# Edge sort of a four-layer graph network: chunks of seven written-out steps in place of a ring of eight looped steps

## The reference, cut to what matters

```python
src, dst, attr, kind      # 412500 edges: source, destination (sorted), 16 attributes, one of 8 types
# layer 0: msg = emb[kind] @ x[src];            m = segment_sum(msg, dst); GRU cell
# layer 1: msg = x[src] @ (attr @ We + be);     segment_sum(msg, dst) + x + bias
# layer 2: two relational convolutions, each edge weighted by 1 / count(dst, kind)
# layer 3: a sheaf layer, sums by destination and by source
```

## Time and profile before

| | us |
|---|---|
| median of 3 runs | 16641.76 (16610.89 to 16656.3) |
| span of the profiled execution | 16996.1 |
| the sort in it, GpSimd's first scatter to its last | 310 to 6837, 6527 in all |
| layers behind it | about 10159 |
| GpSimd busy, the whole span | 5158.9 (30%) |
| VectorE busy, the whole span | 10824.2 (64%) |
| TensorE busy, the whole span | 11995.3 (71%) |

### The profile page before, as it was taken

How to read it: one execution, slowest core, us unless ns; L and a number is a source line. 1 busy time by engine, 2 the same in 40 slices (tenths; PEclk the granted TensorE clock), 3 DMA queues, 4 the chain that set the end, 5 groups by cost and what they waited for, 6 DMA issues and landing times. The chain is left out here.

```text
span 16996.1 us, 429738 instructions
## 1 busy us (share of the span) xinstructions
PE 11995.3 (71%) x146289; PEld 8312.1 (49%) x146290; DVE 10824.2 (64%) x19718; ACT 8088.7 (48%) x16130; POOL 5158.9 (30%) x4771
## 2 busy tenths in 40 slices
PE   1343443434434344799799998997996999999998
PEld 0111111111111111466688886665664888888887
DVE  3233333333333333688788887887886899999998
ACT  1232433433424234566466664665664555555554
POOL 1656666565664656000111111000000111111111
PEclk8555555555555555899899998999998999999999
DMA  7122222222222222688222222887885222333322
GB/s 208 48 72 59 81 67 66 81 59 71 74 58 79 58 72 82 184 229 229 89 106 106 106 106 95 234 235 198 235 235 126 80 83 83 85 85 84 84 84 71
DMA packets 1721891, 1905.31 MB, mean 112 GB/s; under 512 B 981549, under 2 KB 1429103, under 8 KB 1696207
## 3 DMA queue, kind: packets, MB, share of 16 engines
q1 hardware_dynamic: 1602775, 1863.79, 37.0%
q0 software_dynamic: 116864, 39.75, 1.5%
q10 hardware_dynamic: 2078, 0.15, 0.0%
HBM read 1449.57 MB, written 453.42 MB: 112 GB/s over the span
## 5 line engine op out<-in xcount | busy, mean ns | idle before, releaser
L688 POOL DMA_INDIRECT rec<-sort_ring,sort_idx x3520 | 4042.6, 1148 | 2791.9 <-issue 1469.7
L1381 DVE TENSOR_TENSOR e_full<-e_feats,e_masks 128x3840 bf16<-128x3840 bf16 x1179 | 2523.7, 2154 | 350.5 <-ACT e_feats L1339 302.0
L1294 PE MATMUL e_acc<-e_full,e_sel 128*128 128x384 bf16 (+1 forms) x11760 | 2120.9, 327 | 270.4 <-DVE e_full L1381 270.2
L778 PE MATMUL sort_ps_count<-sort_hot,upper_b 128*128 x400 | 231.6, 579 | 2689.9 <-DVE sort_hot L903 2144.6
L1530 PE MATMUL e_acc<-e_outer,e_sel 128*128 128x272 f32 x7840 | 1896.8, 397 | 3.9 <-DVE e_outer L1625 3.9
L1337 ACT CAST e_masks<-e_kind 128x1280 bf16<-128x1280 fp8e4 x1179 | 1482.6, 1258 | 629.5 <-DVE e_full L1381 575.0
L731 ACT CAST sort_cols_t<-sort_ps_late 120x256 f16<-120x256 f32 x98 | 39.5, 403 | 3439.8 <-remote 2373.0
L1530 PEld LDWEIGHTS e_acc<-e_outer,e_sel 128*128 128x128 f32 x7840 | 1459.2, 190 | 281.2 <-issue 4.1
L953 DVE TENSOR_TENSOR sort_over<-sort_ps_late,sort_late_base 128x20 f32<-128x20 f32 x175 | 30.7, 176 | 2428.1 <-remote 2208.7
L1294 PEld LDWEIGHTS e_acc<-e_full,e_sel 128*128 128x128 fp8e4 x11760 | 1061.0, 97 | 933.2 <-issue 298.1
L751 ACT ACTIVATE sort_made<-sort_ps_count,sort_window_bias 128x1024 fp8e4<-128x1024 f32 (+1 forms) x1274 | 1378.7, 1156 | 71.9 <-remote 26.7
(11 more groups left out here) (463 smaller groups left out, 22855.8 us busy)
## 6 DMA issues: line engine op xcount, KB each, us to landing
e_hot<-stream SPq DMA_DIRECT2D x888, 480.0 KB, 3.8
stream<-sort_made SPq DMA_DIRECT2D x98, 2568.0 KB
e_sel<-stream SPq DMA_DIRECT2D x1176, 160.0 KB, 2.7
e_st<-stream SPq DMA_DIRECT2D x99, 1888.0 KB, 7.3
sheaf_gather<-stream SPq DMA_DIRECT2D x393, 384.0 KB, 3.1
e_hot<-stream SPq DMA_DIRECT2D x294, 448.0 KB, 3.5
tail<-sort_made SPq DMA_DIRECT2D x98, 660.0 KB
sheaf_by_dst<-tail SPq DMA_DIRECT2D x491, 128.0 KB, 3.0
```

What stands on the lines that cost most here:

```text
L688: nc.gpsimd.indirect_dma_start(out=rec[q], out_offset=bass.IndirectOffsetOnAxis(ap=idx[:, s, q, c:c + 1], axis=0), in_=ring[:, s, q, c, :] ...
L1294: last = mm(acc[h][:, 0:cols_all], now[:, n * P:(n + 1) * P], full[q & 1][:, n, :], start=j == 0, stop=j == NT - 1)
L1381: v.tensor_tensor(full[q & 1][:, :, 0:cols].rearrange("p j (t k f) -> p j t k f", t=TYPES, k=3), feats[q & 1][:, :, :, :].unsqueeze(2).to_ ...
```

## The change

A quad's steps are done in chunks of `STEPS = 7`. The loop over steps becomes a loop over chunks, and in VectorE's, TensorE's and GpSimd's programs the seven steps of a chunk are written out. `ring`, `idx` and `keys` have two sides, each of 35 tiles for each of the four blocks, and GpSimd's loop takes two chunks in a round. The attributes lie in memory as the kernel's partitions take them, already 21 words wide, so that one DMA a block and chunk loads them (four a chunk); ScalarE writes the keys of the whole chunk with four instructions, and the one and the four fields with five. The pads go. `scattered` counts chunks. The last `find` of a quad, whose result nobody used, goes too. The rows of the odd blocks and their windows move to partitions 32 to 34 (`rows_all`, `windows`). Cut to its core:

```diff
-RING = 8
+STEPS = 7
+CT = STEPS * C
-        ring = sb("ring", [P, RING, Q, C, RW])
-        idx = sb("idx", [P, RING, Q, C], I32)
-        keys = sb("keys", [P, RING, Q, C])
+        ring = sb("ring", [P, 2, Q, CT, RW])
+        idx = sb("idx", [P, 2, STEPS, Q, C], I32)
+        keys = sb("keys", [P, 2, Q, CT])
-        rows = [sb(f"rows{h}", [3, NT, 2, P], F16) for h in range(2)]
+        rows_all = sb("rows", [SECOND + 3, NT, 2, P], F16)
+        rows = [rows_all[at:at + 3, :, :, :] for at in (0, SECOND)]
-        def place_of(i):
-            return bass.ds(i & (RING - 1), 1)
+        def side_of(i):
+            return bass.ds(i & 1, 1)
...
                         for q in range(Q):
-                            sp.dma_start(ring[:, place_of(i), q, :, 0:D].squeeze(1),
-                                         edges[:, tiles(t0[q] + local(i, i0) * C, C), :]).then_inc(attr_in, 16)
+                            sp.dma_start(ring[:, side_of(i), q, :, :].squeeze(1), attr[:, chunk_tiles(t0[q], i, i0), :])\
+                                .then_inc(attr_in, 16)
...
-                    sp.wait_ge(scattered, i1 + RING)
+                    sp.wait_ge(scattered, i1 + 2)
...
+                def scatter(side, chunk, rounds, first):
+                    pool.wait_ge(fields_ready, chunk + 1)
+                    pool.sem_inc(passed, 1)
+                    for s in range(STEPS):
+                        pool.wait_ge(idx_ready, chunk * STEPS + (s + 1))
+                        pool.sem_inc(passed, 1)
+                        for c in range(C):
+                            at = s * C + c
+                            set_of = (at + side) & 1
+                            before_it = rounds + (at + side * ROUNDS >> 1) * (16 * Q)
+                            if not first or at > 1:
+                                pool.wait_ge(landed[set_of], before_it)
+                                if at == 1:
+                                    pool.sem_inc(scattered, 1)
+                                else:
+                                    pool.sem_inc(passed, 1)
+                            for q in range(Q):
+                                nc.gpsimd.indirect_dma_start(
+                                    out=rec[q], out_offset=bass.IndirectOffsetOnAxis(ap=idx[:, side, s, q, c:c + 1], axis=0),
+                                    in_=ring[:, side, q, at, :], in_offset=None).then_inc(landed[set_of], 16)
+                scatter(0, 0, 0, True)
+                with pool.Fori(0, pairs) as u:
+                    scatter(1, u * 2 + 1, u * (ROUNDS * 16 * Q), False)
+                    scatter(0, u * 2 + 2, u * (ROUNDS * 16 * Q) + ROUNDS * 16 * Q, False)
...
                     with act.Fori(i0, i1) as i:
                         act.wait_ge(scattered, i + 1)
+                        for q in range(Q):
+                            last = nc.scalar.activation(keys[:, side_of(i), q, :].squeeze(1), e.key[:, chunk_tiles(t0[q], i, i0)],
+                                                        ACT.Identity, bias=key_bias[:, bass.ds(n, 1), q:q + 1].squeeze(1))
+                        last.then_inc(keys_ready, 1)
+                        act.wait_ge(attr_in, i * (16 * Q) + 16 * Q)
+                        nc.scalar.copy(ring[:, side_of(i), :, :, D:D + 1].squeeze(1).squeeze(3), ones)
+                        for q in range(Q):
+                            last = nc.scalar.copy(ring[:, side_of(i), q, :, D + 1:D + 5].squeeze(1),
+                                                  e.fields[:, chunk_tiles(t0[q], i, i0), :])
+                        last.then_inc(fields_ready, 1)
...
-                def count(a):
-                    now = bass.ds(a & 1, 1)
+                def count(a, s):
+                    now = slice(s & 1, (s & 1) + 1)
...
-                    count(i0 + n)
                     with pe.Fori(i0, i1) as i:
-                        count(i + n + 1)
-                        count_late(i)
+                        a = i * STEPS
+                        count(a, 0)
+                        for s in range(STEPS):
+                            if s + 1 < STEPS:
+                                count(a, s + 1)
+                            count_late(a, s)
...
-                    find(i0, n)
                     with dve.Fori(i0, i1) as i:
-                        find(i + 1, n)
-                        place(i, n)
-                    dve.sem_inc(taken, 1)
+                        a = i * STEPS
+                        dve.wait_ge(keys_ready, i + 1)
+                        dve.wait_ge(scattered, i + 1)
+                        find(i, a, 0)
+                        for s in range(STEPS):
+                            if s + 1 < STEPS:
+                                find(i, a, s + 1)
+                            place(i, a, s)
```

182 lines of the change are left out of this document (72 added, 110 removed).

## The result

| | us |
|---|---|
| predicted | 15994 (15400 to 16700) |
| kernel before, median of 14 | 16672.14 (16599.06 to 16756.08) |
| kernel after, median of 14 | 16534.72 (16447.87 to 16627.1) |
| ratio | 0.9916, 95% interval 0.9896 to 0.9935 |
| span of the profiled execution after | 16449.1 |

The change makes the kernel faster by 137 us. Sign and range hold, the size doesn't: 648 us were forecast, in a band of 15750 to 16350. The two profiles differ by more, 16996.1 against 16449.1, and all of it lies in the sort: behind GpSimd's last scatter come 10168 us (16449.1 - 6281.0), where there were 10159.

A forecast was written before the change was run, and what follows sets the result against it. The sort was taken as bound by a chain of waits, with VectorE getting updates late; 27 us a quad over 24 quads gave 648 us, 16348 profiled, less 354.3 for 15994 us timed, range 15400 to 16700.

The forecast's parts named there:

- The floor: GpSimd's own pace in the sort, 209 us a quad; helping VectorE could gain at most 52 to 53 us a quad.
- The rival's loss of 1250 us: Rival for the sort: stalls shrink until GpSimd never runs dry and bounds the kernel; 15392 us, chance 0.22.
- My remark that timed runs would be under 15730: Check on the sort's stalls: if they came from profiling alone, timed runs would be under 15730 us; the lowest was 16610.89.
- The direct items: VectorE's steps: dropping the eighth find saves 1.7 us a quad, its TensorE matmuls nothing, constant addresses 3 us.
- The signs that I named for being right: Profile after: L903 175 times, 3500 scatters, late-count idle under 2000 us, GpSimd's `idx` wait about halved, 235 us a quad.
- The short stall of the second step, 4.5 us: VectorE's 4.74 us wait for late counts in a quad's second step goes, as ScalarE and SyncE issue a seventh.
- The three long stalls, 18 us: VectorE's late-count waits, some 90 us a quad, shrink by a fifth as TensorE issues twelve fewer address computations a step.
- 27 us a quad: Sum of savings in the sort, 1.7 + 3 + 4.5 + 18, taken over 24 quads as 648 us.
- The timed runs lie 354.3 us below the profiled one, which I take as unchanged: Whole kernel: the gap between 16641.76 timed and 16996.1 profiled was carried over to the kernel after.
- The attribute DMAs: SyncE's loads, one a block and chunk: larger pieces gain nothing, later arrival hides; 0 in the sum.
- pauses for fetching the longer loops: Loop ends: 1.74 us each; one more a quad on VectorE, TensorE and ScalarE costs 125 us, giving 16119.
- The slower rival: Sort: GpSimd's pauses go, late updates are never cleared, a fourth step stalls; +23 us a quad, 17180 us, chance 0.17.

The follow-up runs named there:

- e16: The kernel after, unchanged, in the group of runs without stalls: 15723 us, 0.9982 of the kernel before, which took 15750 us there.
- e7: The kernel before with GpSimd writing only the records of the first of a quad's four blocks, a quarter of the scatters: 14258.30 us, 0.8548 of before.
- e6: The kernel after with GpSimd writing only the records of the first of a quad's four blocks, a quarter of the scatters: 14023.57 us, 0.8407 of before.
- e3: The kernel after with SyncE's and ScalarE's share in seven pieces again (28 attribute DMAs a chunk, nine ScalarE instructions a step): 0.9773 of before at 16917 us.
- e12: The kernel after with SyncE's and ScalarE's share in seven pieces, run again beside the kernel after: 16444.72 us, 0.9887 of before.
- e2: The kernel after with TensorE's half of the counters worked out from a register again, twelve address computations a step: 0.9934 of before at 16917 us.
- e17: The kernel after with six more matmuls and six more weight loads a step, in a group with stalls: 1.0218 of before.
- e10: The kernel before, unchanged, profiled again in one group with the kernel after: median 16665.49 us, 1.0015 of before.
- e11: The kernel after, unchanged, in one group with the kernel before: median 16534.76 us, 0.9939 of before.
- e18: The kernel after with GpSimd beginning a chunk only when four of its seven columns of row numbers are there, in a group with stalls: 0.9862 of before.
- e8: The kernel after with the steps of quad n + 2, in place of quad n + 1, ahead of the blocks of quad n: 1.0105 of before.

## Why the prediction was wrong in size, step by step

- **The floor: right.** I had GpSimd's pace at 209 us a quad; e16 has 211.6. In that group it bounds the kernel after, and by the times the kernel before as well, which no rival had. The rival's loss of 1250 us fits it all the same: 16996 - 1250 is 15746, and 15723 and 15750 were measured; its 15392 was lower by the 354 us. My remark that timed runs would be under 15730 if stalls were a matter of profiling alone can be read now: there is a group in which the kernel before starts at 15732 and the kernel after at 15706, so whether there are stalls depends on the group of runs.
- **The direct items: right.** 1.7 and 3 us for the eighth find and the constant addresses, 4.7 together. Without stalls the steps lose 6.0 us (e7, e6). The blocks lose another 5, which I hadn't seen.
- **The signs that I named for being right** came for the most part: L903 175 times, 3500 scatters, idle time before the read under 2000 us. They speak of the steps alone. The two that speak of the whole quad did not come: 242 us and not 235, and GpSimd's pauses 57.9 to 36.9 us a quad, not halved.
- **The short stall of the second step, 4.5 us: gone in most quads, but worth less.** In the first profile of before it exceeds 2 us in 19 of 25 quads, in that of after in 2. Its mean was 2.5 us and not the 4.74 of the quad that I had read, and it is 2.3 after, since it is 27 and 31 us long in those two. That it went because ScalarE and SyncE issue less is not shown: e3 and e12 issue as much as before and stall least, but their scattering starts later.
- **The three long stalls, 18 us: the size was fair, the reason wrong.** With the 4.5 I expected 22.5 us a quad less idle time before the read; within one group it is 29 (2166 to 1452 us, over 25). But I took out the register items, and with them back the full stalls of e2 are no longer. That a stall is longer the more was issued before it had no row behind it when I wrote it; e17 bears it out, for matmuls. What does lengthen a full stall is matmuls and weight loads (e17), and of these the change takes twelve pairs a quad, the eighth count, which I had put at nothing since it "lies beside VectorE's work". At 2.8 us a pair that is 34 us. That this is what shortened the stalls is argued from e17, no run shows it alone. Why they begin two steps later than before is open.
- **The step that failed: "27 us a quad".** I added up what leaves the steps and took the sum for what leaves the quad. 37 us left the steps, and the blocks got 29 us longer (e10, e11), so the quad lost 8 in the profiles and 3 to 6 in the times. GpSimd has its 209 us of scattering to do in every quad, and what isn't done beside the steps is done beside the blocks, whose ScalarE and TensorE then wait for each other: idle time before L743 283.8 after and before L751 71.9 before in the groups of the first profiles. With a quarter of the scatters the same blocks take 108 us after and 113 before (e6, e7), so it is the scattering beside them that costs. No part of my sum had a term for that, though the earlier trace rows showed a GpSimd with 100.80 us of its scattering beside the steps and 59.48 beside the blocks: shorter steps move scattering over to the blocks. In the quick quad after it is 40.92 and 123.16. The table says what would have been the right quantity: a quad is 202 to 208 us plus GpSimd's pauses in every kernel that scatters all, so a change gains what it takes off the pauses, here 6 us (41.9 to 35.7). That is an account of where the time goes; it doesn't say what sets the pauses. The sum of the stalls doesn't do: e3, e12 and e18 have 574, 697 and 810 us of it, under 40% of e10's, and their quads of 239.6 to 241.5 us are about as long as that of e11 with 1452.
- **"The timed runs lie 354.3 us below the profiled one, which I take as unchanged": wrong**, and it was named as such a risk. The profile is of a level at which a quad takes 263 us, the times are of one at which it takes 248.5. It didn't carry the size of the gain, but it hid the true start: a forecast made from e10's profile with my own 648 us would have been 15982, as wrong.
- **The attribute DMAs: as forecast off the chain.** GpSimd starts 3.1 us after the first row numbers in the quick quad (3125.3 and 3128.39), which is the median of all quads; before it was 1.2. Of pauses for fetching the longer loops I can find none on the chain: the steps of e16 are 36 us for 33.43 of VectorE's work. The Trainium skill's rule of the taken branch ("Runtime: NRT & Kernel Launch", Instruction fetch mechanics) may hold, but it changes nothing that can be seen in these rows.
- **The slower rival** was wrong for this change, because the pauses at a chunk's start stayed (35.7 us against 41.9). Its core, that GpSimd's pauses let the others catch up, fits e6 and e7: with a quarter of the scatters the others' work of a quad takes 144 and 155 us, beside all of them 241 and 249. No run takes the pauses away at a level with stalls: e8 was to do it and has longer ones.

## What to carry to other kernels

Before you add up waits that a change removes, ask what the engine behind them will do in that time, and give the stage that it now runs beside a term of its own: here 37 us left the steps and 29 came back in the blocks. Where two engines slow each other, move the overlap to the stage that bears it best and try starting points in between: with GpSimd waiting for four of seven columns the kernel is at 0.9862 of before, with no such wait at 0.992 to 0.994, with a wait for all seven at 1.0060, and where there were no stalls the wait for four cost 22 us. And compare a profile only with times of the same group of runs, and look where in its group the profiled execution lies: the same kernel took 15750, 16642 or 16917 us, two of these levels stand beside one chip number, and e11's profile is of its fastest execution.

## What the runs showed of the hardware

- One kernel has three levels: medians of before of 15750, 16627 to 16676 and 16917 us, each steady within a group of runs. The difference lies in the sort: behind the last row numbers the kernel after needs 10272 to 10323 us at the middle level and 10421 at the fastest, where GpSimd's last scatter comes 274 us after them and not 105. The number of the chip doesn't decide it: 12 stands beside 16917 and 16676 us, 9 beside 16642 and 15750. What does, no run tells.
- At the two slower levels the news of a finished matmul reaches VectorE up to 46 us late while GpSimd scatters, and up to 61 us with six more pairs of matmul and load a step, 2.8 us a pair. At the fastest level, and with a quarter of the scatters, the delay is nil. Registers' work on TensorE doesn't add to a full stall (45.0 us in e2, 44.9 in e11); whether it adds to their sum is open.
- What holds the items back is open. That something reads them off one by one could also be the recording of the execution. The Trainium skill, "NOTIFIC — the notification-queue block" (Overflow: three behaviours, one of which stalls the engine), says that this block's inner pipeline holds its producers back rather than lose a record, and in its section "Constraints, capacities, measured rates" that emitting an implicit record costs the engine no cycles. No run here was made without recording, so none shows which of the two holds in this case.
